# Slot attention's scan with banks and buffers by role, and the pair levels three levels behind the next slot's scores

## The reference

```python
def step(carry, xs):
    Sk, Sv = carry
    q_t, k_t, v_t, w_t, g_t, b_t = xs
    gt = jnp.exp(g_t)
    bw = b_t[:, :, None] * w_t
    Sk = Sk * gt[:, :, None, :] + k_t[..., :, None] * bw[:, :, None, :]
    Sv = Sv * gt[..., None] + bw[..., None] * v_t[:, :, None, :]
    s = jnp.einsum('bhd,bhdm->bhm', q_t, Sk) * SCALE
    a = jax.nn.softmax(s, axis=-1)
    o_t = jnp.einsum('bhm,bhmd->bhd', a, Sv)
    return ((Sk, Sv), o_t)
```

## Time and profile before

| | us |
|---|---|
| median of 3 runs | 2870.08 |
| profiled execution, its own time | 2872.95 |
| its span, first to last instruction | 2871.2 |
| the four scans together | 910.5 |

### The profile page before, as it was taken

How to read it: one execution, slowest core, us unless ns; L and a number is a source line. 1 busy time by engine, 2 the same in 40 slices (tenths; PEclk the granted TensorE clock), 3 DMA queues, 4 the chain that set the end, 5 groups by cost and what they waited for, 6 DMA issues and landing times. The chain is left out here.

```text
span 2871.2 us, 50901 instructions
## 1 busy us (share of the span) xinstructions
PE 2417.7 (84%) x18448; PEld 1657.8 (58%) x18448; DVE 1727.8 (60%) x3474; ACT 1184.5 (41%) x2881; POOL 1053.2 (37%) x1265
## 2 busy tenths in 40 slices
PE   6888788887888878888747999998889959999989
PEld 3477644776447764477634666666533436666675
DVE  4766676666766667667535676651357546766612
ACT  3644345443454434544313444431115425444401
POOL 0167611676116761167503444420030024444400
PEclk9999989999999999999878999998889979999989
DMA  2100001000010000000012000000100030000000
GB/s 50 41 2 2 2 15 33 2 2 2 15 34 2 2 2 15 15 2 3 2 47 64 17 16 16 5 6 0 46 0 1 1 104 18 16 16 11 5 1 15
DMA packets 74983, 46.64 MB, mean 16 GB/s; under 512 B 27416, under 2 KB 68256, under 8 KB 74400
## 3 DMA queue, kind: packets, MB, share of 16 engines
q1 hardware_dynamic: 74784, 43.95, 5.5%
HBM read 42.89 MB, written 1.05 MB: 15 GB/s over the span
## 5 line engine op out<-in xcount | busy, mean ns | idle before, releaser
L1448 POOL TENSOR_TENSOR rot<-q_plain,ropes 128x512 f32<-128x512 f32 x66 | 83.6, 1266 | 704.6 <-ACT q_plain L1470 704.6
L1045 DVE SCALAR_TENSOR_TENSOR work<-four,taps_g,work 128x511 f32<-128x511 f32 (+2 forms) x384 | 284.2, 747 | 92.0 <-ACT work L789 81.9
L554 PE MATMUL four<-xT,wring 128*128 128x512 f32 x512 | 259.9, 635 | 7.0 <-DMA wring<-in_Ww_dram 4.9
L1419 DVE TENSOR_REDUCE nmaxf<-four 128x1 f32<-128x512 f32 (+3 forms) x256 | 125.8, 491 | 163.1 <-PE four L1345 159.3
L1488 ACT ACTIVATE pr<-four,nmaxf 128x512 f32<-128x512 f32 (+3 forms) x256 | 134.0, 526 | 175.7 <-DVE nmaxf L1419 172.5
L1343 PE MATMUL four<-rot,rot 128*128 128x512 f32 (+3 forms) x512 | 188.3, 463 | 10.8 <-ACT oT L1283 5.6
L1451 POOL TENSOR_TENSOR rpart<-q_plain,ropes 64x512 f32<-64x512 f32 x132 | 167.3, 1267 | 10.4
L789 ACT ACTIVATE work<-four,taps_g 128x512 f32<-128x512 f32 x128 | 88.1, 688 | 180.6 <-PE four L554 180.3
L952 POOL TENSOR_TENSOR work<-work 128x256 f32<-128x256 f32 x184 | 123.4, 670 | 95.2 <-PE bank L641 46.9
L961 POOL TENSOR_TENSOR work<-work 128x256 f32<-128x256 f32 x184 | 141.6, 769 | 38.0 <-DVE work L1099 10.9
L554 PEld LDWEIGHTS four<-xT,wring 128*128 128x128 f32 x512 | 99.3, 206 | 95.8 <-issue 86.8
(11 more groups left out here) (275 smaller groups left out, 5688.3 us busy)
## 6 DMA issues: line engine op xcount, KB each, us to landing
wqkv<-in_f_wq_dram SPq DMA_DIRECT2D x34, 128.0 KB, 2.2
wqkv<-in_f_wk_dram SPq DMA_DIRECT2D x34, 128.0 KB, 2.3
wqkv<-in_f_wv_dram SPq DMA_DIRECT2D x34, 128.0 KB, 2.3
wo<-in_f_wo_dram SPq DMA_DIRECT2D x2, 2048.0 KB, 11.4
we<-in_f_we_dram SPq DMA_DIRECT2D x4, 1024.0 KB
wring<-in_Ww_dram SPq DMA_DIRECT2D x4, 512.0 KB, 4.0
wring<-in_Wk_dram SPq DMA_DIRECT2D x4, 512.0 KB, 4.0
wring<-in_Wv_dram SPq DMA_DIRECT2D x4, 512.0 KB, 3.7
```

The lines of the kernel that those rows point to most:

```text
L554: last = nc.tensor.matmul(k.bank[i % 3][:], wring[n % 2][:, c, h * P:(h + 1) * P], k.xT[:, c, b * T:(b + 1) * T], start=(c == 0), stop=(c ...
L1045: ins = nc.vector.scalar_tensor_tensor(out=cbuf[i % 4][:, s:], in0=k.bank[i % 3][:, 0:T - s], scalar=taps_g[:, {"q": 0, "k": 1}.get(kind, ...
L1419: nc.vector.tensor_reduce(nmax[:, n:n + 1], k.bank[2 + i % 2][:, 0:(qt + 1) * P], AX.X, ALU.max, negate=True).then_inc(s_max, 1)
```

## The change

It rewrites the scan of slot attention alone; the instructions that compute are nearly the same in number and shape.

- Banks by purpose: 0 the transposed keys (`KEY_TURNS`), 1 the scores, slots and state keys (`TURNS`), 2 and 3 the score products in turn (`SCORES`), 4 and 5 the pair products and the states in turn (`PAIRS`), 6 the query-key product, 7 the outputs. All slots use the same banks.
- Buffers by purpose: one U for keys and one V for values (before, U[b] held both in turn), three S and three EE (by s % 3), two acc and two UT7 (by s % 2), one PT and one PD. `tmp` now lies in `DG`, and `state_score` multiplies in place in S. The squares of the outputs go to SK.
- Order: a turn of the loop is seven steps j, each with `score(now, j)`. `pair(mid, j - 3)` runs in steps 3 to 6 and `pair(old, j + 4)` in steps 0 to 2, that is three levels behind. One key transpose stands in each step: levels 3 to 7 of `now` in steps 0 to 4, levels 1 and 2 of `new` in steps 5 and 6. The softmax is spread: `turn_scores(mid)` and `maximum` in step 0, exponentials in step 1, `normalise` and `turn_slots` in step 2, `own_pair` and `outputs(old)` in step 3, the states in step 4, the query-key product and the state keys in step 5, `state_score` and the next slot's `own_score` in step 6.
- Two copies that opened U and S for a slot (L981, L986 on GpSimd) move to ScalarE (`begin_keys`, `begin_reach`).
- New waits come with the single buffers: `begin_keys` and level 0 of the keys wait for the last key transpose of the slot before, and the copy of key level 7 into UT7 waits for `state 1` of the slot two before.
- The loop has 11 turns instead of 10, the first with steps 4 to 6 of `new` alone.

```diff
-AHEAD = 3
-TURNS = [event for c in range(CH)
-         for event in [(c, ("decayed", l)) for l in range(1, AHEAD + 1)] + [(c - 1, "keys")] * (c > 0)
-         + [(c, ("decayed", l)) for l in range(AHEAD + 1, LEVELS + (c < CH - 1))] + [(c, "scores"), (c, "slots")]]
-PRODUCTS = [(c, what) for c in range(CH)
-            for what in ["own score"] + [("score", l) for l in range(LEVELS)] + ["state score"] * (c > 0)
-            + ["own pair"] + [("pair", l) for l in range(LEVELS)]
-            + ["state 0", "state 1"] * (c < CH - 1)]
...
+SLOTS = B * CH
+LAG = 3
+FREE = 3
+def place(s):
+    return s % B, s // B
 def in_flight(s):
+    return tuple(n if 0 <= n < SLOTS else None for n in (s - 2, s - 1, s, s + 1))
+def levels_turned(s):
+    return LEVELS - (s // B == CH - 1)
+def keeps_state(s):
+    return s // B < CH - 1
+KEY_TURNS = [(s, l) for s in range(SLOTS) for l in range(1, levels_turned(s) + 1)]
+TURNS = [event for s in range(SLOTS + 2) for event in
+         [(s - 1, "scores"), (s - 1, "slots")] * (1 <= s <= SLOTS) + [(s - 2, "keys")] * (s >= 2 and keeps_state(s - 2))]
+SCORES = [(s, what) for s in range(SLOTS) for what in ["own"] + list(range(LEVELS)) + ["state"] * (s >= B)]
+PAIRS = [event for s in range(SLOTS + 2) for old, mid in [(s - 2, s - 1)] for event, there in
+         [((old, 4), old >= 0), ((old, 5), old >= 0), ((old, 6), old >= 0), ((mid, "own"), 0 <= mid < SLOTS), ((mid, 0), 0 <= mid < SLOTS),
+          ((old, "state 0"), old >= 0 and keeps_state(old)), ((mid, 1), 0 <= mid < SLOTS),
+          ((old, "state 1"), old >= 0 and keeps_state(old)), ((mid, 2), 0 <= mid < SLOTS), ((mid, 3), 0 <= mid < SLOTS)] if there]
+CHAIN_W = [(s, l) for s in range(SLOTS) for l in range(levels_turned(s))]
+CHAIN_V = [(s, l) for s in range(SLOTS) for l in range(LEVELS - 1)]
+CHAIN_S = [(s, l) for s in range(SLOTS) for l in range(LEVELS - (s < B))]
...
+        key_bank, turn_bank, qk_bank, out_bank = k.bank[0], k.bank[1], k.bank[6], k.bank[7]
+        def score_bank(*what):
+            return k.bank[2 + SCORES.index(what) % 2]
+        def pair_bank(*what):
+            return k.bank[4 + PAIRS.index(what) % 2]
...
+                    def turn_keys(s, l):
+                        i = KEY_TURNS.index((s, l))
+                        pe.wait_ge(chain_w, order(CHAIN_W, g, s, l - 1))
+                        if l == 1:
+                            pe.wait_ge(keys_begun, g * SLOTS + s + 1)
+                        if i:
+                            pe.wait_ge(key_kept, g * len(KEY_TURNS) + i)
+                        for h in range(HG):
+                            last = nc.tensor.transpose(key_bank[:, h * P:(h + 1) * P], U[:, h], k.eye[:])
+                        last.then_inc(key_turned, 1)
...
+                    def score_free(s, what):
+                        i = SCORES.index((s, what))
                         if i >= 2:
+                            pe.wait_ge(score_used, g * len(SCORES) + i - 1)
+                        return b3(score_bank(s, what))
...
+                    def pair_free(s, what):
+                        i = PAIRS.index((s, what))
+                        if i >= 2:
+                            pe.wait_ge(pair_used, g * len(PAIRS) + i - 1)
+                        return pair_bank(s, what)
...
+                    def pair(s, l):
+                        if l:
+                            pe.wait_ge(chain_p, order(CHAIN_S, g, s, l - 1))
+                            pe.wait_ge(chain_v, order(CHAIN_V, g, s, l - 1))
+                        else:
+                            pe.wait_ge(reached, g * SLOTS + s + 1)
+                        out = pair_free(s, l)
...
+                    for s in range(-1, SLOTS + 2):
+                        old, mid, now, new = in_flight(s)
+                        for j in range(LEVELS):
+                            if now is not None:
+                                score(now, j)
+                                if j == LEVELS - 1 and now >= B:
+                                    state_score(now)
+                                if j + LAG <= levels_turned(now):
+                                    turn_keys(now, j + LAG)
+                            if new is not None and j >= 5:
+                                turn_keys(new, j - 4)
+                            if j == 2 and old is not None:
+                                pair(old, 6)
+                            if j == 2 and mid is not None:
+                                turn_slots(mid)
+                            if j == 3 and mid is not None:
+                                own_pair(mid)
+                            if j == 3 and old is not None:
+                                outputs(old)
+                            if j == 4 and old is not None and keeps_state(old):
+                                state(old, 0)
+                            if j == 5 and old is not None and keeps_state(old):
+                                turn_state(old)
+                            if j == 5 and new is not None:
+                                products(new)
+                            if j < 2 and old is not None:
+                                pair(old, j + 4)
+                            if j >= LAG and mid is not None:
+                                pair(mid, j - LAG)
+                            if j == 4 and old is not None and keeps_state(old):
+                                state(old, 1)
+                            if j == 0 and mid is not None:
+                                turn_scores(mid)
+                            if j == LEVELS - 1 and new is not None:
+                                own_score(new)
...
+                    def keep_keys(s, l):
+                        act.wait_ge(key_turned, order(KEY_TURNS, g, s, l))
+                        if l == LEVELS and s >= 2:
+                            act.wait_ge(pair_made, order(PAIRS, g, s - 2, "state 1"))
+                        nc.scalar.activation(turned_keys(s, l), b3(key_bank), ACT.Copy).then_inc(key_kept, 1)
+                    def begin_keys(s):
+                        if s:
+                            act.wait_ge(key_turned, order(KEY_TURNS, g, s - 1, levels_turned(s - 1)))
+                        nc.scalar.activation(halves(U, 0)[:, :, :, 1], halves(chunk(wT, s), 0)[:, :, :, 1], ACT.Copy).then_inc(keys_begun, 1)
...
+                    for s in range(-1, SLOTS + 2):
+                        old, mid, now, new = in_flight(s)
+                        for j in range(LEVELS):
+                            if j == LAG + 1 and old is not None:
+                                if old < B:
+                                    keep_state(old, 0)
+                                for h in range(HG):
+                                    square_out(old, h)
+                                if old < B:
+                                    keep_state(old, 1)
+                            if now is not None and j + LAG <= levels_turned(now):
+                                keep_keys(now, j + LAG)
+                            if j == 4 and new is not None:
+                                begin_keys(new)
+                                begin_reach(new)
+                            if j >= 5 and new is not None:
+                                keep_keys(new, j - 4)
+                            if j == 1 and mid is not None:
+                                exps(mid)
+                            if j == 1 and old is not None:
+                                keep_pair(old, 5)
+                            if j == 2 and old is not None:
+                                assemble(old)
+                                keep_pair(old, 6)
+                            if j == 2 and mid is not None:
+                                keep_slots(mid)
+                            if j in (3, 4) and now is not None:
+                                copy_masked(now, j + 2)
+                            if j == 3 and old is not None:
+                                keep_out(old)
+                            if j == 5 and old is not None and keeps_state(old):
+                                keep_state_keys(old)
+                            if j == LEVELS - 1 and new is not None:
+                                keep_own(new)
...
+                    for s in range(-1, SLOTS + 2):
+                        old, mid, now, new = in_flight(s)
+                        for j in range(LEVELS):
+                            if j == 4 and new is not None:
+                                widen(new, 0)
+                                decay_keys(new, 0)
+                                widen(new, 1)
+                            if j > 4 and new is not None:
+                                decay_keys(new, j - 4)
+                                widen(new, j - 3)
+                            if now is not None and (now, j + LAG) in CHAIN_W:
+                                decay_keys(now, j + LAG)
+                            if now is not None and j + LAG + 1 < LEVELS:
```

(80 more changed lines are left out.)

635 lines of the change are left out of this document (241 added, 394 removed).

## The result

The changed kernel takes 2941.91 us (median of 4 runs, 2936.41 to 2951.58), the kernel before 2870.31 in the same comparison: ratio 1.0252, 95% interval 1.022 to 1.0283. The forecast was 2885, in a range up to 2922; the time lies above the range. The direction was right, the size was not: 72 us where 15 were worked out.

A forecast was written before the change was run, and what follows sets the result against it. No engine is full; handovers in a fixed order bound a slot. Full slots of 28.0 us and the scan ends gave +3.6 a scan, +14.4 on 2872.95, less 2.9 for the median: 2885 us, range 2830 to 2922.

The forecast's parts named there:

- the three waits: Full slot: VectorE for the reach, about 2 us; TensorE before `state 1`, about 0.9; next key transpose behind ScalarE, about 0.45.
- step 5: Slot's end: VectorE finishes pair 3 and mask 0 before TensorE's next score 0; 2.45 us with that score and a handover.
- some 20.1: Lower bound of a full slot in us: TensorE's work alone, with none of the waits of parts 2 and 3.
- the sentence on the clock: In the slots: granted clock stays at 0.99 to 1.00 of full speed, TensorE as busy as before.
- steps 3 and 4: Slot's step 6: GpSimd's next-slot keys then reach, 1.95 us; then VectorE's state score, own_keys and a handover, 2.15.
- Step 2: TensorE from turn_slots to the next slot's second key transpose: 12.98 us of work, 14.35 with two new waits.
- The doubt about VectorE's adds: VectorE and GpSimd share a port pair; with more overlap adds could cost more, 1.6 us a slot at most.
- step 1: Start of a full slot: VectorE runs loop steps 0 to 2 without a gap, 7.05 us.
- The ends of a scan: Slots 0 and 1 gain, slot 2's scores begin at 40.5 us; last maximum +2.2, after it +1.4.
- A: Rival, faster: GpSimd's turn in step 6 does not reach VectorE; slots of 25.7, 2839 us, or 24, 2805. Chance 0.27.
- B: Rival, clearly slower: shared banks and late ScalarE copies make TensorE wait; slots of 29.8, 2921 us. Chance 0.17.
- C: Rival, no change: the gain of slots 0 and 1 pays for the five full ones; 2862 to 2879 us. Chance 0.20.

The follow-up runs named there:

- e2_fill: Changed kernel plus 16 extra TensorE products into the idle output bank in step 6, ahead of own_score: 2916.71 us, ratio 1.0174.
- e1_reach_first: Changed kernel with GpSimd's step 6 decaying the present slot's level 6 reach ahead of the next slot's keys: 2898.86 us, ratio 1.0101.
- e3_own_first: Changed kernel with own_keys and the next slot's first two masks ahead of the state score in VectorE's step 6: 2875.03 us, ratio 1.0027.
- e5_reach_own_states: Changed kernel with the edits of e1_reach_first, e3_own_first and the adjacent states together: 2845.57 us, ratio 0.9924.
- the adjacent states: Changed kernel with a slot's two state products next to each other, ahead of pair 1, on all engines; alone 2936.18 us, ratio 1.024.
- e7_all: Changed kernel with e1_reach_first, e3_own_first, the adjacent states, and normalise, turn_slots and the slots' copy earlier in step 2: 2835.28 us, ratio 0.9889.

## Why the prediction was wrong

The layout of a full slot, step by step, against the timeline (246.07 to 276.54, first mask to first mask):

| step of the forecast | forecast | measured |
|---|---|---|
| 1. VectorE, steps 0 to 2 | 7.05 | 7.26 |
| 2. TensorE, turn_slots to the second key transpose | 14.35 | 15.25 |
| 3. GpSimd, keys then reach | 1.95 | 1.97 |
| 4. VectorE, state score and own_keys | 2.15 | 2.14 |
| 5. to the next first product | 2.45 | 3.79 |
| sum | 28.0 | 30.4 |

**The path was right.** The order of the handovers, the place of each of the three waits and their sizes held: 2.38 us of VectorE for the reach (about 2 predicted), 0.76 before `state 1` (0.9), 0.23 behind ScalarE (0.45). It was read from the new order and the old durations alone. Only step 5 went another way: the forecast has score 0 wait for VectorE's pair 3 and mask 0, and in the timeline it starts behind own_score on TensorE. (The lower bound of TensorE's own work, "some 20.1", adds up to 19.9 from its terms; nothing rests on it.)

**The step that failed is the sentence on the clock,** "The granted clock in the slots is 0.99 to 1.00 of full speed, and TensorE stays as busy." The forecast's own steps 3 and 4 made TensorE stand still for almost 4 us at the end of every slot, where its longest wait in the slots before was 2.7, and I did not put those together. TensorE's duration rows were taken at the upper clock, and in step 5 the first two batches behind the gap run at the lower one. So the failed term is step 5, put at 2.45 us and measured at 3.79. In e2_fill, with the clock kept up, the same step takes 2.22 (from the end of own_keys at 266.74 to the mask at 268.96), so the clock costs 1.57 there. Of the 57 us that the kernel lies above the forecast this is 22 us by the times. In the profiled executions the scans lie 66.8 us above the forecast (991.7 for 910.5 + 14.4): 35.9 by the clock in the twenty slots, 7.9 by everything else in them (568.7 in e2_fill, 560.8 forecast), and 23.0 at the ends of the scans. The clock is the largest single term, not the whole miss. The rows that should have warned me were there: the clock is 0.95 over the whole scan and 0.99 over its seven slots, so at the scan's two ends it was (0.95 x 225.9 - 0.99 x 182.5) / 43.4 = 0.78; taken apart, 1.00 before the first maximum and 0.57 behind the last, where weight loads fill 8.8 of 23.7 us.

**Unlike batches stand further apart than like ones.** Step 2 was put 0.9 too short, though its two waits were even over-priced (1.35 against about 1.0). Its work took some 14.2 us in place of 12.98. The distances between starts, read in the timeline: own pair 0.53 behind a transpose batch, taken as 0.44; pair 0 behind the outputs 1.98, taken as 1.78; levels 4 and 6 and the query-key product 0.99 to the next batch and the states 0.96, each taken as 0.88 from the like batches in the earlier trace rows. The last transpose, on whose end GpSimd waits, ends 0.60 after its start, taken as 0.44.

The doubt about VectorE's adds did not come true: they take 442 ns in slots 2 to 6 (503 before). The product of the slots with the gates in own_pair (L1177) takes 981 ns instead of 693, and normalise (L1166) 779 instead of 692; the latter is part of step 1. Why, no run shows.

**The ends of a scan.** Here the forecast was most wrong in proportion. Score 0 of slot 2 was put at 40.5 us after the start and came at 46.4 (TensorE at 185.15). Nearly all of the difference is slot 1, 25.2 us from score 0 to score 0 where 19.8 was laid out. The timeline:

```profile
159.99 1.83 PE L684 MATMUL four<-work,bw 128*128 128x128 f32 x8
...
168.46 0.18 DVE L1164 RECIPROCAL sums<-sums 128x4 f32<-128x4 f32 x1 [0.64 <-ACT work L876]
...
169.91 1.54 PE L684 MATMUL four<-work 128*128 128x128 f32 x8
...
174.33 2.08 PE L684 MATMUL four<-work 128*128 128x128 f32 x8
...
177.41 0.85 POOL L1003 TENSOR_TENSOR work<-wT,gT 128x256 f32<-128x256 f32 x1 [1.29 <-PE four L633]
```

Score 0 and levels 3 and 4 run at the lower clock in whole or in part: score 0 one batch behind a stop of 2.02 us, level 3 one transpose behind a stop of 3.03, and level 4 with the clock not yet back. GpSimd then waits 1.29 us for the transpose behind level 4. VectorE's steps 0 to 2 take 7.4 us where 5.7 was laid out, with three waits in them (0.50 for the turned scores, 0.52 for the reach, 0.64 for the exponentials). The load of the exponentials' table (1.28 us at 165.55) stands in that chain, as it did in the kernel before (at 159.75). In the later scans the interval between the first two maxima is 23.1 to 23.2 us instead of 24.6, so the first scan shows this end at its worst. From the last maximum to the last copy it is 25.65 us, where 24.5 was forecast and 23.1 measured before. Together, for the first scan: 5.9 up to slot 2, 149.7 against 140.2 in five slots, 1.6 in slot 7, 1.1 behind it: 18.1 us of the miss. Which share the clock has in the ends no run tells apart, since e2_fill fills only the stops of slots 2 to 6.

**The rivals.** A said that a slot would be 25.7 without the wait for the reach. e1_reach_first, which takes most of that wait away and nothing else, gives 27.2 with the clock up; e3_own_first, which fills it, gives 26.6, and e5_reach_own_states, with both and the adjacent states, 24.7. Its mechanism was the real lever, but the order as written forbids it, as the text said. B named 29.8 a slot for coupling through banks and ScalarE. The size came near (30.5), the cause did not: e1_reach_first and e3_own_first change neither bank nor ScalarE, and take 43 and 65 us of 72 away. C, that the gain of slots 0 and 1 pays for the rest, fell with that gain: the first maximum comes 24.9 us after the start, 19.7 before.

**The rule on the most contended engine.** The Trainium skill ("Perfetto Trace Analysis", Identifying the Most-Contended Engine) points to the engine with the highest occupancy. No run here shows an engine at its bound: a full slot of e7_all, 24.1 us, still has 19.8 of weight loads, and every gain but e2_fill's came from an order of handovers. The same page's Matmul Optimizations says that the matmul engine scales its power with utilization, and asks for matmuls back to back in batches. e2_fill agrees: 22 us gained by products that nobody reads.

**The lag and the roles themselves** were not undone in a run of their own. What e7_all shows is that with another order in steps 2, 4 and 6 they allow slots 2 us shorter than before, while a scan's first maximum comes 25.0 us after its start (164.9 - 139.9), where it was 19.7, and from the last maximum (330.9) to the end of the last copy (358.0) it is 27.1 us, where it was 23.7. In the first scan the seven intervals save 16.4 us (166.1 for 182.5), and the two ends give 8.7 of them back. That is why 2 us a slot give only 1.1%. e3_own_first shows the same: its seven intervals sum to 704.7 us in four scans, 28 less than before (733.1), and yet it is 8 us slower, with 25.0 us before the first maximum and 26.5 behind the last.

## What to carry to other kernels

When work of the next unit is woven into the current one, look in each in-order queue for an operation of the next unit that stands in front of one that the current unit still needs: `decay_keys` before `decay_reach` and the state score before own_keys were two such places, and turning the second round, three calls, won back 65 of 72 us by itself. Lay out the chain with the new order before believing that spreading a head over steps hides it, and where that layout leaves TensorE idle for some 4 us, price the batches behind the gap at the lower clock, and for 2 us give both prices. When an edit's gain seems to change with what stands beside it, compare the difference with the intervals and sum the same stretches in both profiles before believing it: the adjacent states looked like 3 us in one comparison and 12 in the other, and were 5.5 and 5.6 in the slots.

## What was not expected of the hardware

After a stop of 3.79 us TensorE's clock fell to the lower level (eight matmuls in 2.08 and 1.75 us, 1.16 at the upper level) behind all twenty such stops of the profiled execution, for both batches in 18 of them and for the second alone in two. Here is one of the two:

```profile
332.94 1.16 PE L674 MATMUL four<-work,bw 128*128 128x128 f32 x8 [3.79 <-DVE work L1119]
...
333.94 1.70 PE L684 MATMUL four<-work,bw 128*128 128x128 f32 x8
```

Behind stops of 2.08 us it fell in ten slots and not in the ten others of one execution (e1_reach_first). Filling the stop with products (3.8 us of them) kept a slot's mean granted clock at 1.00 and shortened the slot by 1.6 us, although TensorE then had 23.4 us of weight loads in it, for 19.7 in a slot of e1_reach_first at the same clock.
